# Context attention of a decoder layer: the first fill of the spare PSUM bank stands ahead of the turn of the probabilities in even steps

## The reference

```python
def _L0_xattn_ref(query, key, value, mask, w_q, b_q, w_k, b_k, w_v, b_v, w_o, b_o):
    q = query @ w_q.T + b_q
    k = key @ w_k.T + b_k
    v = value @ w_v.T + b_v
    q, k, v = (a.reshape(B, S, H, D_K).transpose(0, 2, 1, 3) for a in (q, k, v))
    scores = jnp.einsum('bhqd,bhkd->bhqk', q, k)
    scores = jnp.where(mask[:, None, :, :] == 0, jnp.float32(-1000000000.0), scores)
    scores = scores / jnp.sqrt(jnp.float32(D_K))
    attn = jax.nn.softmax(scores, axis=-1)
    ctx = jnp.einsum('bhqk,bhkd->bhqd', attn, v)
    return ctx.transpose(0, 2, 1, 3).reshape(B, S, H * D_K) @ w_o.T + b_o

x = _layernorm(x + _L0_xattn_ref(x, ctx_1024, ctx_1024, mask, ...), axis=-1)
```

## Time and profile before

| What | Value |
|---|---|
| median of 3 runs | 960.47 us (960.2 to 961.97) |
| profiled execution, its own time | 962.27 us |
| its span in the trace | 960.5 us, 1.8 us less |
| mean granted TensorE clock | 0.976 of full speed |
| busy share of the span | PE 88%, PE weight loads 57%, DVE 73%, ACT 56%, POOL 56% |
| steps 0 to 63 of the context attention | about 256 to 480 us of the span |

### The profile page before, as it was taken

How to read it: one execution, slowest core, us unless ns; L and a number is a source line. 1 busy time by engine, 2 the same in 40 slices (tenths; PEclk the granted TensorE clock), 3 DMA queues, 4 the chain that set the end, 5 groups by cost and what they waited for, 6 DMA issues and landing times.

```text
span 960.5 us, 17027 instructions
## 1 busy us (share of the span) xinstructions
PE 849.7 (88%) x5581; PEld 549.5 (57%) x5581; DVE 698.2 (73%) x1834; ACT 535.3 (56%) x1390; POOL 533.1 (56%) x599
## 2 busy tenths in 40 slices
PE   4599999998699989988878999989988989999993
PEld 2244444444466556565545666657555656798762
DVE  3888888886577777776867775875887588375687
ACT  3477777784577677667544444543444354464331
POOL 4688888887610111101346675653858887763673
PEclk9799999999889999999999999999999999999997
DMA  7300000000131111000122221221122125444221
GB/s 225 99 1 1 0 1 0 1 1 0 38 91 50 51 50 40 1 2 1 31 50 53 59 56 40 53 59 47 45 51 78 55 69 157 150 144 154 56 55 45
DMA packets 57847, 51.86 MB, mean 54 GB/s; under 512 B 11586, under 2 KB 43042, under 8 KB 57762
## 3 DMA queue, kind: packets, MB, share of 16 engines
q1 hardware_dynamic: 55234, 46.06, 17.4%
q0 software_dynamic: 2304, 4.72, 1.7%
q10 hardware_dynamic: 224, 0.01, 0.0%
HBM read 21.66 MB, written 12.32 MB: 35 GB/s over the span
## 4 chain that ended last, share of the span: by engine, by line
PE 55%; DVE 18%; POOL 13%; issue 6%; ACT 6%; SPq 1%; DMA 0%; POOLq 0%; ACTq 0%; DVEq 0%
PE psum L1920 6%; PE psum L1887 5%; PE psum L2048 4%; PE psum L1949 4%; PE psum L2122 3%; PE psum L2256 3%; PE psum L2236 3%; POOL area L816 3%; PE psum L1866 3%; PE psum L1872 3%; PE psum L2219 2%; DVE area L1364 2%; PE psum L2200 2%; DVE negmax L1386 2%; PE psum L1784 2%
## 5 line engine op out<-in xcount | busy, mean ns | idle before, releaser
L905 POOL TENSOR_TENSOR area<-area,rinv 128x512 f32<-128x512 f32 x64 | 94.1, 1470 | 87.2 <-DVE rinv L1678 86.8
L1364 DVE SCALAR_TENSOR_TENSOR area<-psum,ccol,cs 128x512 f32<-128x512 f32 x128 | 89.9, 744 | 49.8 <-PE psum L1920 49.7
L1189 ACT ACTIVATE area<-psum,negmax 128x128 f32<-128x128 f32 (+1 forms) x256 | 104.0, 423 | 27.7 <-DVE negmax L1379 27.6
L1386 DVE TENSOR_REDUCE negmax<-psum 128x2 f32<-128x512 f32 x128 | 82.3, 685 | 39.6 <-PE psum L1872 39.5
L1049 ACT ACTIVATE area<-psum,negmax 128x256 f32<-128x256 f32 x256 | 101.6, 506 | 0.0
L1920 PE MATMUL psum<-area,qkw 128*128 128x512 f32 x128 | 73.7, 658 | 26.8 <-DVE area L1364 5.0
L1177 ACT ACTIVATE area<-psum 128x512 f32<-128x512 f32 x32 | 19.1, 598 | 119.9 <-PE psum L2256 119.9
L745 POOL TENSOR_TENSOR ve<-mv,eps_o 128x2 f32<-128x2 f32 x8 | 1.7, 213 | 141.1 <-DVE mv L1338 141.1
L1887 PE MATMUL psum<-ident,area 128*128 128x128 f32 x512 | 71.8, 282 | 2.0 <-ACT area L1059 2.0
L1379 DVE TENSOR_REDUCE negmax<-psum 128x2 f32<-128x512 f32 (+1 forms) x128 | 64.8, 547 | 4.8 <-PE psum L1949 4.8
L2048 PE MATMUL psum<-area 128*128 128x512 f32 x128 | 63.6, 601 | 1.1
(11 more groups left out here) (303 smaller groups left out, 2108.4 us busy)
## 6 DMA issues: line engine op xcount, KB each, us to landing
area<-area SPq DMA_DIRECT2D x256, 64.0 KB, 2.0
slot_out<-area SPq DMA_DIRECT2D x17, 256.0 KB, 2.3
area<-slot_in SPq DMA_DIRECT2D x8, 512.0 KB, 4.0
slot_in<-gate SPq DMA_DIRECT2D x5, 768.0 KB, 4.6
area<-in_L_ffn_re_w SPq DMA_DIRECT2D x14, 256.0 KB, 3.3
area<-in_mask_BxSxS_ik SPq DMA_DIRECT2D x8, 256.0 KB, 4.5
area<-in_L_attn_W SPq DMA_DIRECT2D x5, 256.0 KB, 6.4
area<-in_x SPq DMA_DIRECT2D x4, 256.0 KB, 3.0
```

The lines of the kernel that those rows point to most:

```text
L905: pool.tensor_tensor(p4, p4, rinv[:, u % 4, 0:4].unsqueeze(2).to_broadcast([128, 4, w]), ALU.mult)\
L1189: last = act.activation(Pc[:, u % 4, r, mm, 0:w], psum[:, 2 * (u % 2) + r, mm * w:(mm + 1) * w], ACT.Exp, bias=negmax[:, u % 4, r, mm:mm + 1],
L1364: last = nc.vector.scalar_tensor_tensor(rp[:, w, j, :].rearrange("p (b n) -> p b n", b=2), bank[7].rearrange("p (b n) -> p b n", b=2), cco ...
L1386: nc.vector.tensor_reduce(out=negmax[:, n % 4, r, :], in_=bank[2 * (n % 2) + r].rearrange("p (m k) -> p m k", m=2), axis=mybir.AxisListTyp ...
```

## The change

In a step with even n, the early fill of the spare bank is issued between `scores` and `turn`, no longer behind `turn`. DVE's step follows: it reads the early fill of an even step before it copies half 0 of the turn. Odd steps stay as they are. The lists of ACT, POOL and SyncE are the same as before.

```diff
@@ DVE, context_step(n)
+                if n % 2 == 0:
+                    for what, fb in fills(n, EARLY):
+                        read_fill(what, fb)
                 if 0 <= n - 1 < XN:
                     v = n - 1
                     if v >= 4:
                         dve.wait_ge(x_pv, v // 2 - 1)
                     dve.wait_ge(x_t, 2 * v + 1)
                     nc.vector.tensor_copy(PT[:, v % 4, 0, :], bank[4]).then_inc(x_pt[0], 1)
-                for what, fb in fills(n, EARLY) + fills(n, LATE):
+                for what, fb in (fills(n, EARLY) if n % 2 else []) + fills(n, LATE):
                     read_fill(what, fb)
@@ PE, context_step(n)
                 if 0 <= n + 2 < XN:
                     scores(n + 2)
+                if n % 2 == 0:
+                    for what, b in fills(n, EARLY):
+                        fill(what, b)
                 if 0 <= n - 1 < XN:
                     turn(n - 1)
-                for what, b in fills(n, EARLY):
-                    fill(what, b)
+                if n % 2:
+                    for what, b in fills(n, EARLY):
+                        fill(what, b)
```

## The result

The changed kernel takes 951.4 us (median of 4 runs, 948.6 to 952.5), the kernel before 961.1 us in the same comparison (4 runs, 960.2 to 962.0). The ratio is 0.990, 95% interval 0.988 to 0.992: faster by 1.0%, 9.7 us. Forecast were 949.6 us and 10.9 us less.

What follows compares the result with a forecast made beforehand. PE was taken to bound the context stage, busy 202 of 224 us. Terms 4.50 + 3.54 + 1.98 + 1.20 - 0.35 = 10.87 us gave a forecast of 949.6 us from 960.47, range 946.5 to 955.5.

Steps and rivals of the forecast that it cites:

- u = 4: tokens1's wait on PE for ACT's reading of rows_q1: 0.75 us gained each, six times, 4.50 us.
- u = 6: out's wait on PE for DVE's reading of values: 0.59 us gained each, six times, 3.54 us.
- rival c: No change: another chain, for instance KS in the next odd step, takes the freed time; 960.5 us, chance 0.06.
- rival d: Slower: scores or turns wait for the later turn's copies, 18.1 us lost against 10.9 won; 967.7 us, chance 0.07.
- Rival b: More than forecast: PE's whole idle time in four wait rows, 14.9 us, goes; 945.6 us, chance 0.05.
- Rival a: Small margins in u = 4 and u = 2 give part back; gain 5.5 to 9, 951.5 to 955, chance 0.20.
- u = 0 to 2: Earlier fills of inputs and rows_q0: 0.33 us six times (1.98), and 0.24 five times (1.20).
- the later of the two, by 0.07: In u = 4, PE's fill and turn end at 359.15, behind ACT freeing tokens1 at about 359.08.
- The 1.09 us: Time DVE's copy in u = 6 would hold the engine by the skill's DRAIN rule; sum 2.9 us larger.
- they can come 0.37 earlier, which passes on the 0.33 of the term before: ACT's squares in u = 1, bound by DVE's normalised tokens at 375.00, pass the 0.33 us on to u = 2.
- the 0.24 for u = 2: ACT's idle time ahead of reading rows_q0, won on top in five batches, 1.20 us.
- The first batch: No late fills, so no wait removed; 0.17 us lost in step 2, 0.18 in step 6, 0.35 in all.

Runs made afterwards that it cites:

- e1: Kernel before, with the early fill ahead of the turn only in steps with u = 4; 995.8 us against 999.0, regular batch 27.75 us.
- e2: Changed kernel with DVE's old order (copy, then values), so PE's swap alone; 993.4 us, regular batch 27.4 us.
- e3: Kernel before with only the DVE half of the change, PE's order as before; 999.9 us against 999.0, regular batch 28.27 us.
- e4: Changed kernel, with POOL's subtraction in u = 1 waiting until DVE has written the normalised tokens; 992.3 us, regular batch 26.40 us.
- e6: Kernel before, with the early fill ahead of the turn only in steps with u = 2; 962.1 us against 960.3, regular batch 28.23 us.
- e12: The changed kernel timed once more, against the kernel before; 950.5 us against 959.7, ratio 0.990.
- e9: Changed kernel, but first batch as before, plus e4's wait and DVE reading KS's fill before half 0's copy in u = 3, 5; 945.4 us.
- e10: As e9, and in u = 3 and u = 5 PE too issues the fill of rows_k ahead of the turn; 947.6 us, ratio 0.987.

## Why the prediction was right

**The mechanism.** Two fills of one bank stood next to each other, and the turn between them hides the reader. That is what e1 (u = 4) and e2 with e3 (u = 6) show, and no rival took over. Neither KS (rival c) nor a turn waiting for a copy (rival d) has a new row in the regular batches of the changed kernel. Rival b needed all waits to go; 2.8 and 1.5 us of them stayed. Rival a came true in one place only, u = 0 to 2, and not from the small margins that I named for it.

**The terms.** By the steps' lengths:

- u = 4: 0.83 us each, 5.0 in all; forecast 0.75 and 4.5. The mis-sized step is PE's own path: the prediction let the turn start 0.67 us behind the fill, a distance read where other work follows, and its weights started 0.48 behind (354.01 to 354.49). So PE is not "the later of the two, by 0.07". The weights of tokens1 begin at 355.43, which is 0.05 behind the end of ACT's reading (354.78 + 0.60 = 355.38), as before the change (359.86 to 359.91); the turn's weight loads come 0.11 us apart, and the next was due at about 355.35. ACT's reading ends last there, by less than 0.1 us, and the prediction's sum for ACT (0.78 + 0.60 + 0.05 = 1.43 us) is what the pair takes, 1.42.
- u = 6: 0.60 each, 3.6; forecast 0.59 and 3.5. The 1.09 us that the prediction works out beside the rows do not apply. The Trainium skill, "VectorE: DVE Perf Modes", section "The DRAIN you can't avoid", adds that a next instruction that is not held starts earlier, and the pitch of 0.60 us fits that. So the trace does not contradict the section, as the prediction has it.
- u = 0 to 2: 0.38 in each of five batches (0.34 in u = 1, 0.09 in u = 2, less 0.04 in u = 0) and 0.45 in the batch without rms, 2.4 in all; forecast 1.98 + 1.20 = 3.2. The step that failed is "they can come 0.37 earlier, which passes on the 0.33 of the term before". The squares came 0.05 us earlier in their step, not 0.37, as the normalised tokens took 0.97 us, not 0.59. The change itself made that collision, by an earlier reading of inputs and so an earlier start of POOL. I had priced ACT's earlier work and not looked at what it starts on a third engine. e4 gives back 0.37 us a batch. With it u = 0 to 2 win 0.75, more than the 0.57 forecast: the 0.24 for u = 2 was too small as well (0.36 in e6), which the collision hid.
- The first batch: steps 2, 6 and 7 are longer by 0.03, 0.05 and 0.12, 0.2 us in all; forecast 0.35. Step 6 with its turn in step 7 was right; in step 2 the keys were hardly waited for.

The sum is 5.0 + 3.6 + 2.4 - 0.2 = 10.8 us, against 10.87 forecast. The gain of u = 4 was set 0.5 us too low and the first batch's loss 0.15 too high, u = 0 to 2 were set 0.8 too high, and that they cancel is luck.

**What lay outside.** The profiled executions differ by 9.8 us, 1.0 less than the stage. The trace shows where. The first and the last of ACT's copies of that kind in self attention, before and then after:

```profile
L1177 ACT ACTIVATE area<-psum x32: 592/597/601, 518.3 to 833.9; 128x512 f32<-128x512 f32 x32
```

```profile
L1177 ACT ACTIVATE area<-psum x32: 592/597/602, 509.6 to 824.1; 128x512 f32<-128x512 f32 x32
```

At the first the lead is 8.7 us, at the last 9.8; in between it changes only near 710 to 730. The granted clock of two stretches, first before, then after (the last three figures: clock, DMA share, GB/s):

```profile
500.00:550.00 50.00, 44.33 (x322) 29.07 (x322) 38.06 (x87) 23.67 (x99) 31.82 (x27) 1.00 0.23 56
...
700.00:750.00 50.00, 44.82 (x339) 29.88 (x338) 39.59 (x101) 18.94 (x74) 34.60 (x28) 0.97 0.23 59
```

```profile
490.00:540.00 50.00, 44.93 (x315) 29.07 (x316) 36.87 (x84) 23.33 (x97) 29.62 (x25) 0.95 0.22 53
...
690.00:740.00 50.00, 44.34 (x349) 29.83 (x348) 40.98 (x102) 19.90 (x79) 35.38 (x29) 1.00 0.24 62
```

Both executions had a dip of the clock just behind the stage. Before, the clock was 0.83 from 490 to 500 us and full from 500; in the changed kernel it was 0.75 from 480 to 490 and 0.73 from 490 to 500. The longer dip goes with a loss of 1.8 us (a lead of 10.5 at the last scores, 8.7 at the first copy). The kernel before had another, 0.83 from 710 to 720, which goes with 1.2 us the other way. The dips belong to the execution and not to the kernel: e12, the same kernel as the changed one, had the full clock from 480 to 500 and its first copy at 505.8 us, not 509.6. What sets them off stays open.

## What to carry to other kernels

Where one buffer is used twice in a row on the engine that sets the pace, put work between the uses that needs neither, and order the reader likewise: in u = 6 PE's swap won nothing without DVE's (e2), and DVE's alone half (e3). After an instruction has moved up, follow what its reader starts on the other engines; an engine with time to spare can slow one that has none, and one semaphore wait gave 0.37 of 26.8 us back. When steps repeat exactly, measure step lengths in the trace: they resolve 0.02 us where whole times scatter by 2.

## What the runs showed of the hardware

- A VectorE `tensor_scalar` (128x128, SBUF to SBUF, float32) that meets a GpSimd `tensor_tensor` which started 0.10 us earlier is held until that ends: POOL's row ends at 369.97, where the second of DVE's two instructions starts, and its 0.33 us give the pair's end (369.34 + 0.97 = 370.31). The first takes 0.71 us instead of 0.34, POOL's row 0.73 us with or without the meeting, and so it is in all five batches with rms. All five meet at the same distance, so other ways of slowing are not excluded. It agrees with the Trainium skill, "SBUF — State Buffer", section "Who interferes with whom", by which a VectorE instruction in a mode that uses both ports and a GpSimd instruction exclude each other for the whole length of the first; that this instruction ran in such a mode no run shows.
- The sixteen weight loads of values (32 columns each) are through after 0.59 us, their matmuls (256 columns each) after 1.07, and the next weight load starts 0.41 us after the last of the sixteen, in e9, e10 and the kernel before alike. A gap in the row of weight loads need not be one of the matmuls.
- Consecutive ACT rows that wait for nothing overlap, here by 0.22 us, so the idle time in a row was less than what an earlier release gave: 0.24 shown, the reading's start 0.46 sooner, its end 0.36 (e6).
